# A two-layer kernel whose engine orders are written out as a table of streams, with new planned durations

## Chip, core and metric

The kernel runs on one core of one Trainium2 chip. The metric is device time in microseconds (us), as the median of several executions. TensorE is called PE, VectorE DVE, ScalarE ACT, GpSimd POOL and SyncE SP, as in the profile.

## What is computed

Input is x of shape (4, 1024, 128), that is 4096 tokens of 128 numbers, and the weights of two layers. Each layer normalises x once and adds an attention part and a feed-forward part of the same normalised tensor to x:

```python
xn = layernorm(x)
x = x + rwkv6_attention(xn) + moe_ffn_0(xn)      # first layer
xn = layernorm(x)
x = x + causal_attention(xn) + looped_moe(xn)    # second layer
```

- The recurrent attention (4 heads, key width 64, value width 128) mixes each token with the one before it through five small products, and then runs the recurrence `S = exp(w_t) * S + k_t v_t`.
- `moe_ffn_0` cuts every token into 8 pieces of 16, takes the best 2 of 16 experts for each and applies gelu between two products.
- The causal attention has 16 heads of width 8 with one shared key and value head, over 1024 tokens in each of 4 batches.
- `looped_moe` is run twice: rms-norm, a router, the best 2 of 8 experts (128 to 256 to 128, silu gate), and a sum.

## The kernel before

Everything stays in fp32 or in exact splits into bf16 parts. The work of each layer is written as many **streams**: Python generators, one for each part of the work on each engine. Every generator yields, ahead of each step, the planned start of that step, and `merge` (L63) takes the generators of one engine and always advances the one whose next planned start is smallest. So the planned starts set the order of the instructions on PE, ACT, DVE, POOL and SP. Between the two layers all five queues meet (`k.meet`).

**Where the planned starts come from.** `first_layer` (L2178) and `second_layer` (L2416) describe every step to a `Plan` (L2068): the engine, the stream, a key, a wished time, a duration (`takes`), the steps that it needs, and which PSUM banks it fills or frees. `Plan.run` (L2089) then plays the plan through: again and again it picks the engine that can start soonest and, on it, among the heads of the streams that can start within a small slack, the one with the smallest wish. The result gives the starts (`FIRST` and `AT` in the code) and the bank of every use (`plan.place`).

- The first layer works in four turns of 1024 tokens (`plan_mixtures`, `plan_levels`, `plan_carry`, `plan_gated`), 0 to about 548 us of the trace. Beside them run 256 gelu tiles: PE forms each with two products (L482), ACT applies gelu (L528), PE reduces (L494), DVE weighs (L543), POOL adds (L582).
- In each turn a recurrence of levels runs between PE and DVE. DVE scales (L1121, L1126), PE fills the banks of a level (a small product at L650 and then L737, L764 or L779), and DVE places the result (L1064).
- The mixtures of a turn: PE L673, DVE `rw_mix` L1008, POOL `rw_mix` L1158, then the products L685, L691, L707, L720. POOL also clears `rw_full` once (L1164, step `zero`).
- The second layer holds attention and experts side by side. Attention has a pass for the maxima (PE L2718 and L2736, DVE L2764 or L2761) and one for the sums (PE L2863 and L2840, ACT exp L2887, PE L2826). Experts: PE L3109, L3125, L3141, L3157, ACT L3186, L3198, L3208, DVE L3218, L3232.
- The experts' results go to memory, POOL gathers them (L3049), and DVE adds them to `zt` (L3244, L3249).
- At the start of the second layer DVE turns constants into bf16 (L1821, step `cast`), and `ap_value` (L1980) takes a product from the banks.
- PE works in several tile shapes (128x128, 128x32, 64x128, 32x128 and so on). The plan charges 0.1 us for each change of shape (`TILE_SWITCH`) and 1.3 us for each change of ACT's function table.

## Time and profile before

| | us |
|---|---|
| median of 3 executions | 1351.98 |
| lowest and highest | 1349.23 and 1352.38 |
| profiled execution, first to last instruction (span) | 1317.6 |
| PE busy | 1206.5 (92% of the span) |
| DVE busy | 1050.7 (80%) |
| ACT busy | 891.2 (68%) |
| POOL busy | 482.3 (37%) |

The profile gives the span of its execution; what lies around the span isn't in it, and the median of the three executions is 34.4 us above it. Busy time counts the instructions of an engine; the releaser of a wait is the instruction that ended it. The granted clock is the share of full speed that PE was given.

### The profile page before, as it was taken

The numbers are of one execution on the slowest core, as the hardware profiler recorded it, in microseconds if no ns is written. First come the engines' busy times: TensorE is split into PE (matmuls) and PEld (weight loads), VectorE is DVE, ScalarE is ACT, GpSimd is POOL, SyncE is SP. The second block draws the span as 40 slices with busy tenths as digits, with TensorE's granted clock in tenths as the row PEclk, the third lists the DMA queues.
The fourth block names the chain that finished last, engine by engine and source line by source line (L and its number), as shares of the span: only waits on it lengthen the run. The fifth ranks groups of instructions, "written<-read, shape, count | busy, mean of one in ns | idle before, by whom it ended". The sixth has DMA issues, their size and how long they took to land. (4 is left out here: it accounts for less than half of the span.)

```text
span 1317.6 us, 28397 instructions
## 1 busy us (share of the span) xinstructions
PE 1206.5 (92%) x11172; PEld 593.3 (45%) x11172; DVE 1050.7 (80%) x1954; ACT 891.2 (68%) x1246; POOL 482.3 (37%) x446
## 2 busy tenths in 40 slices
PE   6888998899988989798899999999899999999988
PEld 3333332333433323365555555555456544555434
DVE  4589789869898779769977799778787798787863
ACT  3668997898877888643266676666666666666666
POOL 3542554345514872320155511555025550000170
PEclk8889998999999999989999999999999999999999
DMA  6333322233332343248364544556335453233020
GB/s 224 116 117 125 106 94 101 92 109 101 100 103 94 111 132 106 93 118 233 106 183 136 174 122 117 151 139 157 87 101 160 133 142 89 72 82 105 19 64 28
DMA packets 129876, 152.88 MB, mean 116 GB/s; under 512 B 16048, under 2 KB 90800, under 8 KB 129616
## 3 DMA queue, kind: packets, MB, share of 16 engines
q1 hardware_dynamic: 111104, 127.50, 32.9%
q0 software_dynamic: 8192, 16.79, 4.3%
q10 hardware_dynamic: 10448, 6.77, 1.7%
q8 instruction: 89, 1.46, 0.5%
q14 instruction: 43, 0.35, 0.1%
HBM read 109.20 MB, written 41.81 MB: 115 GB/s over the span
## 5 line engine op out<-in xcount | busy, mean ns | idle before, releaser
L2887 ACT ACTIVATE ax_prob<-second_pair 128x1024 f32<-128x1024 f32 (+1 forms) x320 | 292.9, 939 | 146.4 <-PE second_pair L2840 94.4
L528 ACT ACTIVATE m_act_h<-first_pair,const 128x1024 f32<-128x1024 f32 x256 | 270.1, 1114 | 57.7 <-PE first_pair L482 44.1
L2764 DVE TENSOR_REDUCE am_top<-second_pair 128x2 f32<-128x1024 f32 (+1 forms) x192 | 222.9, 1175 | 38.6 <-PE second_pair L2718 25.5
L3019 POOL DMA_INDIRECT slot_tokens<-xn,mr_slots x128 | 124.0, 969 | 273.7 <-PE second_bank L1877 86.2
L3049 POOL DMA_INDIRECT m_back<-slot_results,mr_slots x128 | 122.2, 955 | 243.2 <-PE second_pair L2718 167.7
L482 PE MATMUL first_pair<-m_terms,w1s 96*128 96x512 bf16 x512 | 145.9, 391 | 19.6 <-ACT m_act_h L528 19.4
L2826 PE MATMUL ax_sums<-ax_prob,al_vs 128*32 128x512 f32 (+3 forms) x1536 | 161.2, 500 | 1.8 <-ACT ax_prob L2887 1.6
L494 PE MATMUL first_pair<-m_act_h,const 128*32 128x512 f32 x1024 | 130.4, 610 | 7.0 <-DVE m_prod L543 4.9
L582 POOL TENSOR_TENSOR m_both<-m_prod,m_both 128x512 f32<-128x512 f32 x64 | 86.7, 1371 | 123.8 <-DVE m_both L543 123.8
L2863 PE MATMUL second_pair<-al_qs,al_ks 51*128 51x512 bf16 (+3 forms) x768 | 115.9, 329 | 12.8 <-DVE am_top L2764 4.3
L2718 PE MATMUL second_pair<-al_ks,al_qs 48*128 48x512 bf16 (+3 forms) x768 | 116.2, 327 | 7.6 <-DVE am_top L2764 3.7
L482 PEld LDWEIGHTS first_pair<-m_terms,w1s 96*128 96x128 bf16 x512 | 38.4, 99 | 136.7 <-ACT m_act_h L528 75.3
L2863 PEld LDWEIGHTS second_pair<-al_qs,al_ks 51*128 51x128 bf16 x768 | 32.9, 93 | 103.8 <-issue 48.0
L2764 DVE TENSOR_REDUCE am_later<-second_pair 128x2 f32<-128x768 f32 (+1 forms) x64 | 68.6, 1085 | 6.4 <-PE second_pair L2736 6.1
L3141 PE MATMUL second_pair<-m_tok,m_wt 128*128 128x256 f32 (+1 forms) x244 | 66.8, 361 | 2.1 <-DVE m_act L3218 1.0
L2718 PEld LDWEIGHTS second_pair<-al_ks,al_qs 48*128 48x128 bf16 x768 | 33.5, 93 | 62.4 <-issue 30.9
L494 PEld LDWEIGHTS first_pair<-m_act_h,const 128*32 128x32 f32 x1024 | 25.9, 110 | 77.4 <-issue 46.3
L3157 PE MATMUL second_bank<-m_wt,m_hid 128*128 128x128 f32 x364 | 60.0, 295 | 0.8 <-DVE m_hid L3232 0.7
L3125 PE MATMUL second_bank<-m_tok,m_wt 128*128 128x256 f32 (+1 forms) x216 | 58.2, 364 | 2.2 <-DMA m_wt<-in_experts 1.6
L1158 POOL TENSOR_TENSOR rw_mix<-rw_mix,xn 128x512 f32<-128x512 f32 x40 | 48.5, 1235 | 23.5 <-DVE rw_mix L1008 23.4
L543 DVE SCALAR_TENSOR_TENSOR m_both<-first_pair,const,m_share 128x512 f32<-128x512 f32 x64 | 46.6, 741 | 11.8 <-PE first_pair L494 10.9
L543 DVE SCALAR_TENSOR_TENSOR m_prod<-first_pair,const,m_share 128x512 f32<-128x512 f32 x64 | 46.8, 740 | 10.5 <-issue 7.8
(396 smaller groups left out, 2515.1 us busy)
## 6 DMA issues: line engine op xcount, KB each, us to landing
m_wt<-in_experts SPq DMA_DIRECT2D x96, 384.0 KB
m_share<-shares SPq DMA_DIRECT2D x128, 256.0 KB
m_rows<-slot_tokens SPq DMA_DIRECT2D x60, 128.0 KB
slot_results<-m_y SPq DMA_DIRECT2D x60, 128.0 KB
stack<-mp_part SPq DMA_DIRECT2D x48, 128.0 KB
m_terms<-stack SPq DMA_DIRECT2D x64, 96.0 KB, 3.7
qstack<-ap_qpart SPq DMA_DIRECT2D x48, 128.0 KB
al_qs<-qstack SPq DMA_DIRECT2D x32, 192.0 KB, 3.9
```

What stands on the lines that cost most here:

```text
L482: p = E.matmul(banks.bank("up", n, ep)[:, j, :], self.w1s[:, (4 * half + ep) * P:(4 * half + ep + 1) * P], self.terms[:, q % slots, :], st ...
L494: p = E.matmul(banks.bank("down", n, j)[32 * ep:32 * ep + 32, :], self.w("w2", 32 * (4 * half + ep), 32 * (4 * half + ep) + 32), self.act_ ...
L528: A.activation(self.act_h[:, slot, :, :], banks.bank("up", n, ep)[:, :, :], ACT.Gelu, bias=self.w("b1", 4 * half + ep, 4 * half + ep + 1)) ...
L543: V.scalar_tensor_tensor(self.product(pair, half, j)[:, :], banks.bank("down", n, j), self.w("b2", half, half + 1), self.share[:, q % slot ...
L582: G.tensor_tensor(both[:, :], self.prod[j][:, :], both[:, :], ALU.add).then_inc(self.folded, 1)
L2718: p = E.matmul(banks.bank("max", i, m)[:, x, first:first + n], *self.keys_queries(i, blk, a, x, seg, n), start=a == pairs[0], stop=True, s ...
L2764: V.tensor_reduce(into[:, 2 * a:2 * a + 2, at], tile[:, :, 0:n], AX, ALU.max, negate=True).then_inc(*banks.empties("max", i, m))
L2826: p = E.matmul(self.sums[VW * h:VW * h + VW, off:TILE], self.loads.vs[:, b % 2, blk, :], self.prob[:, g % 3, h, off:TILE], start=blk == 0, ...
L2863: p = E.matmul(tile[:, x, first:first + n], self.loads.ks[rows, b % 2, blk * CH:(blk + 1) * CH], self.loads.qs[rows, i % Q_SLOTS, a, th * ...
L2887: A.activation(dst, src, ACT.Exp, scale=SCALE).then_inc(*banks.empties("sum", i, u))
L3019: G.indirect_dma_start(self.tokens[g], bass.IndirectOffsetOnAxis(ap=self.route.slots[g][second][:, i:i + 1], axis=0), self.entry.zn(GC * g ...
L3049: G.indirect_dma_start(self.back[q % 2][:, n, m, :], None, self.results[ph], bass.IndirectOffsetOnAxis(ap=self.route.slots[g][n][:, c * NC ...
```

## The change

The plan's steps, streams and needs stay, and every instruction stays. What changes:

1. `Plan.run` takes an `orders` table: for each engine a string in which each letter names the stream that takes the next step on that engine (a for the first stream declared, b for the second, and so on). Wishes, slack and patience no longer choose. `FIRST_ORDERS` spells out the first layer and `SECOND_ORDERS` the second.
2. Some 30 planned durations are set to other values, and two planned needs are added (the first load of the attention waits for `zero`, the products for the maxima for `cast`). They no longer choose the order; they move the planned starts along it, and through these the choice of PSUM banks.

```diff
+ENGINES = ["PE", "ACT", "DVE", "POOL", "SP"]
+NAMES = "abcdefghijklmnopqrstuvwxyzABCDEFGHIJKLMNOPQRSTUVWXYZ"
...
-    def run(self):
-
+    def run(self, orders=None):
+
+        spelled = collections.defaultdict(list)
+        for engine, stream in self.streams:
+            spelled[engine].append((engine, stream))
+        turns = {engine: [spelled[engine][NAMES.index(name)] for name in order] for engine, order in (orders or {}).items()}
+        taken = collections.Counter()
...
             for (engine, stream), n in heads.items():
+                if orders and turns[engine][taken[engine]] != (engine, stream):
+                    continue
...
-            engine = min(best, key=lambda e: min(best[e])[0])
+            engine = min(sorted(best, key=ENGINES.index), key=lambda e: min(best[e])[-1] if orders else min(best[e])[0])
+            taken[engine] += 1
...
+FIRST_ORDERS = {
+    "PE":
+        "affaffghgahhigcccigccbajcccgccddkccddccjddcjcjccddcckcackcdccdecbcacddcckcdccddcckcacddcckckdeccddclcecclkccddcckclddllcfmmcbfaccffccddgccec"
...
-    return p.run(), p
+    return p.run(FIRST_ORDERS), p
...
-            pe("levels", ("lev", it, h), at, 1.7 if h < 32 else 1.0, ready, ("zero",), *(ago("outs", 1) if h == 32 else []), lag=0.3, fills=1, uses=[("lev", it, h, s) for s in range(2)])
+            pe("levels", ("lev", it, h), at, 0.87 if h < 32 else 1.0, ready, ("zero",), *(ago("outs", 1) if h == 32 else []), lag=0.3, fills=1, uses=[("lev", it, h, s) for s in range(2)])
...
-        dve("low", ("mixed", it, s), at, 1.24, ("delta", it, s), *([("low", it, 0, 1)] if s else ago("state", NC)), port=True)
+        dve("low", ("mixed", it, s), at, 0.68, ("delta", it, s), *([("low", it, 0, 1)] if s else ago("state", NC)), port=True)
...
-        dve("turn", ("parts", i), end, 1.6, ("rows", i), *([("sent", i - 2)] if i > 1 else []))
+        dve("turn", ("parts", i), end, 1.05, ("rows", i), *([("sent", i - 2)] if i > 1 else []))
...
-            act("exp", ("exp", i, u), wish, {384: 0.75, 128: 0.52}.get(n, 0.95), ("sum", i, u),
+            act("exp", ("exp", i, u), wish, {384: 0.7, 128: 0.49}.get(n, 0.91), ("sum", i, u),
...
-    return p.run(), p
+    return p.run(SECOND_ORDERS), p
```

The order moves on every engine. Three places follow. The lines of the changed kernel stand one higher up to L2060 of the old one, and 75 higher behind the tables.

**POOL, mixtures of the first turn** (`rw_mix` is the mixture, `rw_full` the buffer that is cleared, `mp_` the router of the feed-forward part). Before:

```order
L291 TENSOR_TENSOR mp_h<-mp_h,mp_part 128x512
L294 TENSOR_TENSOR mp_part<-mp_h,mp_part 128x512
L1163 MEMSET rw_carry 128x128
L1164 MEMSET rw_full 128x4096
L1158 TENSOR_TENSOR rw_mix<-rw_mix,xn 128x512 x2
L357 TENSOR_TENSOR mp_logits<-mp_logits,mp_peak 128x512
L1158 TENSOR_TENSOR rw_mix<-rw_mix,xn 128x512 x2
```

After the change:

```order
L1159 TENSOR_TENSOR rw_mix<-rw_mix,xn 128x512 x4
L358 TENSOR_TENSOR mp_logits<-mp_logits,mp_peak 128x512
L361 TENSOR_TENSOR mp_one<-mp_one,mp_eq 128x512
L1159 TENSOR_TENSOR rw_mix<-rw_mix,xn 128x512 x2
L365 TENSOR_TENSOR mp_one<-mp_one,mp_logits 128x512
L369 TENSOR_TENSOR mp_one<-mp_one,mp_sum 128x512
L1159 TENSOR_TENSOR rw_mix<-rw_mix,xn 128x512
L292 TENSOR_TENSOR mp_h<-mp_h,mp_part 128x512
L295 TENSOR_TENSOR mp_part<-mp_h,mp_part 128x512
L1164 MEMSET rw_carry 128x128
L1165 MEMSET rw_full 128x4096
```

Clearing `rw_carry` and `rw_full` stood ahead of the first mixtures, and now stands behind the mixtures of the first turn but three.

**PE, second turn, from the fill of one level to the fill of the next** (`rw_selves` with `rw_key` or `rw_low` are fills; `m_terms` and `m_act_h` belong to the gelu tiles). Before:

```order
L650 MATMUL first_pair<-bf_ident 32x1
L737 MATMUL first_pair<-rw_selves,rw_key 32x64 x32
L482 MATMUL first_pair<-m_terms,w1s 128x512 x4
L494 MATMUL first_pair<-m_act_h,const 32x512 x4
L650 MATMUL first_pair<-bf_ident 32x1
L737 MATMUL first_pair<-rw_selves,rw_low 32x64 x32
```

After the change:

```order
L651 MATMUL first_pair<-bf_ident 32x1
L738 MATMUL first_pair<-rw_selves,rw_key 32x64 x32
L483 MATMUL first_pair<-m_terms,w1s 128x512 x2
L238 MATMUL first_pair<-xn,const 128x512
L483 MATMUL first_pair<-m_terms,w1s 128x512 x4
L495 MATMUL first_pair<-m_act_h,const 32x512 x4
L483 MATMUL first_pair<-m_terms,w1s 128x512 x2
L495 MATMUL first_pair<-m_act_h,const 32x512 x4
L483 MATMUL first_pair<-m_terms,w1s 128x512 x4
L651 MATMUL first_pair<-bf_ident 32x1
L738 MATMUL first_pair<-rw_selves,rw_low 32x64 x32
```

Between the two fills there were 8 products, and there are now 21.

**DVE, near the end of the second layer** (`am_top` and `am_later` reduce scores from PSUM, `m_back` are gathered results, `ao_` belongs to the output projection). Before:

```order
L3259 TENSOR_TENSOR zt<-zt,x 128x512
L2764 TENSOR_REDUCE am_top<-second_pair 128x2
L2764 TENSOR_REDUCE am_later<-second_pair 128x2
L3244 SCALAR_TENSOR_TENSOR zt<-m_back,mr_share,zt 128x128 x4
L3249 SCALAR_TENSOR_TENSOR zt<-m_back,mr_share,zt 128x128 x4
L2764 TENSOR_REDUCE am_later<-second_pair 128x2
L2954 RECIPROCAL ao_inverse<-second_bank 128x16
L2956 TENSOR_TENSOR ao_scaled<-second_bank,ao_inverse 128x128
L2768 TENSOR_TENSOR am_top<-am_top,am_later 128x4x4
L2787 CAST am_part<-am_rows 32x128
L2789 TENSOR_TENSOR am_restm<-am_rows,am_part 32x128
```

After the change:

```order
L2843 TENSOR_TENSOR am_top<-am_top,am_later 128x4x4
L3029 RECIPROCAL ao_inverse<-second_pair 128x16
L3031 TENSOR_TENSOR ao_scaled<-second_pair,ao_inverse 128x128
L2862 CAST am_part<-am_rows 32x128
L2864 TENSOR_TENSOR am_restm<-am_rows,am_part 32x128
L2866 CAST am_part<-am_restm 32x128
L2868 TENSOR_TENSOR am_part<-am_restm,am_part 32x128
L3029 RECIPROCAL ao_inverse<-second_bank 128x16
L3031 TENSOR_TENSOR ao_scaled<-second_bank,ao_inverse 128x128
L3319 SCALAR_TENSOR_TENSOR zt<-m_back,mr_share,zt 128x128 x4
L3324 SCALAR_TENSOR_TENSOR zt<-m_back,mr_share,zt 128x128 x4
L3319 SCALAR_TENSOR_TENSOR zt<-m_back,mr_share,zt 128x128 x4
```

Before, the additions of gathered results (L3244, L3249) stood ahead of a score reduction (L2764) and of the step that ends the maxima (L2768 to L2793). Now the last score reductions stand ahead of the first row shown (L2843 is the old L2768), and the additions (L3319, L3324) behind all of them.

## Rows read from the trace of the kernel before

**Rows 1.** The page's head: busy time, share of the span, instructions.
```profile
PE 1206.5 (92%) x11172; PEld 593.3 (45%) x11172; DVE 1050.7 (80%) x1954; ACT 891.2 (68%) x1246; POOL 482.3 (37%) x446
```

**Rows 2.** Five stretches: length, busy of each engine, granted clock, DMA share, GB/s.
```profile
0.00:66.00 66.00, 48.45 (x261) 22.48 (x269) 34.54 (x64) 31.80 (x44) 29.81 (x26) 0.87 0.54 170
66.00:528.00 462.00, 418.62 (x4144) 157.95 (x4142) 394.37 (x759) 380.24 (x431) 218.58 (x181) 0.98 0.32 106
528.00:660.00 132.00, 112.13 (x731) 71.11 (x730) 108.48 (x227) 55.65 (x110) 23.55 (x21) 0.96 0.48 138
660.00:1254.00 594.00, 574.85 (x5491) 318.76 (x5489) 484.62 (x832) 380.25 (x608) 186.66 (x196) 1.00 0.44 120
1254.00:1317.60 63.60, 52.44 (x565) 23.01 (x557) 28.70 (x76) 43.24 (x54) 23.74 (x25) 0.95 0.17 45
```

**Rows 3.** PE's waits from 66 to 528 us: total, times, longest.
```profile
PE first_pair L482 <- ACT m_act_h L528: 17.3, 40, 1.6
PE first_pair L650 <- DVE rw_low L1126: 7.0, 4, 3.1
PE first_pair L494 <- DVE m_prod L543: 4.9, 3, 2.7
```

**Rows 4.** PE in order of time: start, us, instruction, [idle before <-releaser].
```profile
58.37 0.60 PE L482 MATMUL first_pair<-m_terms,w1s 96*128 96x512 bf16 x2 [0.40 <-ACT m_act_h L528]
```

**Rows 5.** PE between two level fills, second turn.
```profile
218.87 1.06 PE L494 MATMUL first_pair<-m_act_h,const 128*32 128x512 f32 x8
223.00 0.18 PE L650 MATMUL first_pair<-bf_ident 64*32 64x1 bf16 x1 [3.06 <-DVE rw_low L1126]
```

**Rows 6.** DVE in the same stretch.
```profile
219.21 2.55 DVE L1121 SCALAR_TENSOR_TENSOR rw_selves<-rw_pre,const,rw_rec 128x256 f32<-128x256 f32 x2
221.69 1.25 DVE L1126 TENSOR_TENSOR rw_low<-rw_suf,rw_key 128x256 f32<-128x256 f32 x1
...
225.48 1.66 DVE L1121 SCALAR_TENSOR_TENSOR rw_selves<-rw_pre,const,rw_rec 128x256 f32<-128x256 f32 x4
```

**Rows 7.** POOL in the same stretch.
```profile
217.79 2.51 POOL L582 TENSOR_TENSOR m_both<-m_prod,m_both 128x512 f32<-128x512 f32 x2
```

**Rows 8.** DVE groups by line: busy, mean ns of one, idle before.
```profile
L1121 DVE SCALAR_TENSOR_TENSOR rw_selves<-rw_pre,const,rw_rec 128x256 f32<-128x256 f32 x96 | 51.6, 585 | 0.0
```

**Rows 9.** PE in the second layer, score products and an expert's product.
```profile
1100.01 0.38 PE L2718 MATMUL second_pair<-al_ks,al_qs 48*128 48x512 bf16 x2
1100.23 0.38 PE L2863 MATMUL second_pair<-al_qs,al_ks 51*128 51x512 bf16 x2
1100.54 1.16 PE L3157 MATMUL second_bank<-m_wt,m_hid 128*128 128x128 f32 x8
```

**Rows 10.** ACT's table loads at the gelu.
```profile
L528 ACT ACT_TABLE_LOAD x16 | 20.5, 1283 | 0.3
```

**Rows 11.** POOL in the first turn's mixtures.
```profile
41.66 3.50 POOL L1164 MEMSET rw_full<- 128x4096 f32 x1
45.13 2.35 POOL L1158 TENSOR_TENSOR rw_mix<-rw_mix,xn 128x512 f32<-128x512 f32 x2
```

**Rows 12.** PE, the product that waits for them.
```profile
46.49 1.12 PE L685 MATMUL first_pair<-rw_mix,const 128*128 128x512 f32 x2 [2.09 <-POOL rw_mix L1158]
```

**Rows 13.** DVE behind the start of the second layer.
```profile
559.09 0.23 DVE L1821 CAST bf_earlier_t<-const 128x128 bf16<-128x128 f32 x1 [0.89 <-DMA const<-in_const]
```

**Rows 14.** PE in the same stretch.
```profile
561.86 1.92 PE L1885 MATMUL second_pair<-ax_y,const 128*32 128x512 f32 x2 [3.68 <-DVE ap_value L1980]
```

**Rows 15.** DVE near the end.
```profile
1267.54 1.14 DVE L3244 SCALAR_TENSOR_TENSOR zt<-m_back,mr_share,zt 128x128 f32<-128x128 f32 x4 [2.66 <-DMA m_back<-slot_results,mr_slots]
...
1269.64 1.22 DVE L2764 TENSOR_REDUCE am_later<-second_pair 128x2 f32<-128x1024 f32 x1
```

**Rows 16.** PE near the end.
```profile
1270.92 0.39 PE L2863 MATMUL second_pair<-al_qs,al_ks 51*128 51x512 bf16 x2 [2.25 <-DVE am_later L2764]
...
1274.04 1.93 PE L2826 MATMUL ax_sums<-ax_prob,al_vs 128*32 128x512 f32 x8 [0.61 <-ACT ax_prob L2887]
```

More of the change, by code:

```diff
@@ L2256, in plan_units @@
             if half:
-                pool("pair", ("pair", pair, j), at + DOWN_AFTER, 1.3, ("product", n, j))
+                pool("pair", ("pair", pair, j), at + DOWN_AFTER, 1.26, ("product", n, j))
         if n % 4 == 3:
@@ L2320, in plan_levels @@
         dve("scales", ("self", it, h), at, 0.4, ("bonus", it), *ago("lev64", 1), lag=0.15, port=True)
-    pe("levels", ("lev", it, 0), at, 2.2, ("self", it, NH - 1), *ago("fill_a"), lag=0.3, fills=1, uses=[("lev", it, 0, s) for s in range(2)])
+    pe("levels", ("lev", it, 0), at, 1.12, ("self", it, NH - 1), *ago("fill_a"), lag=0.3, fills=1, uses=[("lev", it, 0, s) for s in range(2)])
     for s in range(2):
@@ L2342, in plan_levels @@
     for half in range(2):
-        pe("levels", ("lev64", it, half), at, 1.25, ("scale", it, 64, 2), lag=0.3, fills=1, uses=[("lev64", it, half, s) for s in range(2)])
+        pe("levels", ("lev64", it, half), at, 0.97, ("scale", it, 64, 2), lag=0.3, fills=1, uses=[("lev64", it, half, s) for s in range(2)])
         for s in range(2):
@@ L2379, in plan_gated @@
     for s in range(2):
[L2380 to L2381 removed]
+        dve("gn", ("gngate", it, s), at, 0.67, ("affine", it, s), lag=0.2, port=True)
+        pe("gn", ("go", it, s), at, 0.88, ("gngate", it, s), lag=0.3, fills=1)
     for s in range(2):
@@ L2522, in plan_route @@
             dve("route", ("zn", ph, c), at, 1.1, ("invert", ph))
-        pe("route", ("turned", ph, c), at, 0.75, ("zn", ph, c) if loop else ("scale", GC * g + c), *before, lag=0.25, fills=1)
+        pe("route", ("turned", ph, c), at, 0.5, ("zn", ph, c) if loop else ("scale", GC * g + c), *before, lag=0.25, fills=1)
         act("route", ("turnedc", ph, c), at, 0.48, ("turned", ph, c), *before, frees=("turned", ph, c))
```

102 lines of the change are left out of this document (79 added, 23 removed).

## The prediction

> **What bounds the kernel now.** I read the head of the page first. PE is busy for 1206.5 us of a span of 1317.6 us, DVE for 1050.7 and ACT for 891.2 [rows 1]. No instruction goes away with this change, so it can win PE's idle time, which is 111.1 us, and the time lost to a lower clock, and little else. The table of stretches says where these lie [rows 2]. Each figure is length less PE's busy time:
>
> - 0 to 66 us (normalisation, first mixtures): 17.5 us idle.
> - 66 to 528 us (first layer): 43.4 us idle, granted clock 0.98.
> - 528 to 660 us (the layers meet, the second starts): 19.9 us idle, clock 0.96.
> - 660 to 1254 us (second layer): 19.2 us idle in 594, clock 1.00.
> - 1254 us to the end: 11.2 us idle, clock 0.95.
>
> So the second layer's long middle is bound by PE, and better order has little to find there. In the first layer no engine is full: PE 418.6, DVE 394.4 and ACT 380.2 of 462 us. There the order itself is the limit.
>
> PE's list of waits for the first layer shows two kinds [rows 3]. The first is the gelu: 17.3 us in 40 waits. The order of time shows one. Two products take 0.60 us, one gelu more than that, so a tile formed directly behind others waits 0.40 us for its bank [rows 4]. The second kind is the chain of levels: 7.0 us in only 4 waits in front of L650. The longest shows the mechanism. PE has 8 products between two fills and is done at 219.93, then idles 3.06 us [rows 5]. DVE meanwhile needs 2.55 us for two L1121 and 1.25 us for one L1126, while four L1121 take 1.66 us a little later [rows 6]. POOL works without a break in the slow stretch [rows 7]. So a DVE step between SBUF operands can take some three times its time beside POOL (1.28 us each against 0.42). Over all 96 the mean is 585 ns [rows 8], 170 ns above the 415 of the undisturbed ones, 16 us in total.
>
> **The change, part by part.** The letters spell the same steps, and on every engine the count of instructions of each operation is the same; only ACT's table loads differ. Costs and gains are counted against the profiled execution (span 1317.6). The median of the runs is 34.4 us above that span, and I carry this over unchanged.
>
> *Changes of tile shape.* Counting over the whole order of PE, from shape to shape, the first layer goes from 298 to 338 changes, the second from 735 to 686. A price is in the trace: products with 64 rows start 0.22 us apart, and the last of them before a 128x128 product 0.31 us apart, so 0.09 us for a change [rows 9]. That makes +3.6 and -4.4 us. The Trainium skill (TensorEngine Tiling (Array Packing), Key Properties) says that changing the tiling mode drains the engine; it gives no price, and by that rule alone the first layer would pay for each of its 40 new changes and the time there would rise by those 3.6 us.
>
> *Table loads.* ACT has 42 before and 37 now, all five in the first layer, at 1.28 us each [rows 10]: 6.4 us less on ACT. ACT has 82 us idle there, so I cost it at nothing beside the next term. If gelu were the bound it would be worth the 6.4.
>
> *Start.* POOL clears `rw_full` for 3.50 us and only then makes the first mixtures [rows 11]. PE waits 2.09 us for these [rows 12]. The new order has the mixtures first. I take -2 us, between 0 (the next wait takes its place) and -4. What is late next is `rw_full`, which the steps that place the levels need, later in the turn.
>
> *Gelu waits.* I count the tiles whose two products stand directly behind another tile's: 106 of 256 before, 82 now, 23% fewer. 23% of 17.3 us is 4 us. Bounds 0 and -9 (half).
>
> *Level chain.* Between the fills of the levels of one turn PE now has 757 products instead of 590, over the four turns. At the place that waited 3.06 us it has 21 instead of 8. These waits should nearly go: -6 us of 7.0. Bounds +4 (one gap now holds 2 products, one 5, and each can wait what the longest waits now) and -7.
>
> *The other waits of the first layer.* 43.4 less 17.3 and 7.0 leaves 19.1 us in small waits for DVE, POOL and ACT. I see no single place there, and take a third, -6. Bounds 0 and -12.
>
> *Clock.* A share of 0.02 of 462 us is 9.2 us lost, 0.04 of 132 us is 5.3, and 0.05 of 63.6 is 3.2 [rows 2]. The drops follow stalls, so fewer stalls give back some: -3 in the first layer; those behind it are in the next terms.
>
> *Meeting of the layers.* DVE takes its bf16 constants when their load lands, at 559.09 us, and L1980 stands behind them [rows 13]. PE waits 3.68 us for L1980, with two L1885 in a row, and then takes 1.92 us for one of them, in a stretch of lower clock [rows 14]. In the new order PE has eleven products of the experts and the router between `ap_value`'s product and L1885. -5 us, bounds 0 and -8.
>
> *Middle of the second layer.* 19.2 us of idle time in 594: -3, bounds +6 and -8.
>
> *End.* DVE stands at the addition of gathered results for 2.66 us, with a score reduction behind it [rows 15]. PE waits 2.25 us for that reduction and then takes 1.93 us for eight L2826, twice the time of full clock [rows 16]. The new order has these reductions and the end of the maxima ahead of the additions: -4 us, bounds 0 and -7.
>
> The sum is -2 + 3.6 - 4.4 - 4 - 6 - 6 - 3 - 5 - 3 - 4 = -33.8 us. A removed wait can return at the next place: PE that comes earlier meets the next late producer, here DVE, busy for 85% of the first layer. Of the 30 us of idle time that I take out I give a third back, +10; the third is my choice, between none and all. That leaves -24: a span near 1294 and a median of **1328 us**.
>
> **Rivals.**
>
> *Nearly all of it returns.* The waits move from the old places to new ones, and only the changes of shape remain (-0.8 us): 1351 us. For it: ACT and DVE are over 80% busy in the first layer. Against it: the two structural stalls, DVE behind a gather and POOL behind a memset, have nothing to take their place.
>
> *More is found.* A search over orders for all engines together could halve the idle time behind 66 us, 93.7 us, and with it half of the 17.7 us of clock: -47 -9 + 10 = -46, or 1306 us. Against it: the middle of the second layer has hardly any.
>
> *Slower: DVE beside POOL.* The new plan takes lower times for DVE steps that share with POOL (0.68 for 1.24, 0.67 for 0.9). If PE's order is now cut to DVE steps at full speed, each stretched step is waited for. Of the chains of levels the whole stretch of 16 us (L1121 alone) would show on PE, where 7.0 of waits show now: +9. With the changes of shape in the first layer (+3.6), and two stalls as long as today's longest at the gaps of 2 and 5 products (+6), it comes to +19 with no gain elsewhere: 1371 us. It decides if PE's idle time in the first layer rises above 43.4 us by more than what start, meeting and end give (11). Against it: the gaps grew where the chain waited. The Trainium skill (SBUF — State Buffer, section "SBUF: two separate sides") calls the port pair that DVE and GpSimd share an exclusive lock for a whole instruction. By that rule a DVE step waits out a POOL step; the trace agrees, with 1.28 us against 0.42 beside POOL steps of 1.26.
>
> That the change does nothing is excluded: nearly every row of every engine's order moves.
>
> **How the numbers follow.** A difference below 0.3% (4 us) can't be told from none here. Forecast, 1310 to 1347: 0.65. More is found: 0.15. Nearly all returns: 0.09. Slower: 0.11. The likeliest gives 1328. The range must leave out no more than 2 in 10: from 1304, which takes in most of the larger gain, to 1352, which takes in the case of no change and leaves out the slower one. Faster 0.80, same 0.09, slower 0.11.
>
> **What would show it.** In the profile of the changed kernel: PE's idle time in the first layer near 30 us; waits of L651 under 3 us in total; no wait of PE for POOL's mixtures; no DVE wait for a gather with a score reduction behind it; granted clock 0.99 or more there; PE's busy time within some 10 us of 1206. If PE's idle time is as before, with new waits for DVE at L651 or for gelu at L483, the forecast is wrong and the second or the last rival holds.

## The result, and the profile after

| | before | changed |
|---|---|---|
| median, us | 1352.18 (4 executions, 1349.23 to 1360.16) | 1303.38 (4 executions, 1300.2 to 1305.22) |
| ratio | | 0.9641 [0.9605, 0.9677] |
| profiled execution, its own time | not recorded | 1300.2 |
| its span | 1317.6 | 1298.7 |

The kernel became 48.8 us faster, twice the 24 us of the forecast, and 0.6 us below the range. The direction was right, and the size nearest to the rival "more is found" (1306).

The table holds a trap. The changed kernel's time is its span plus 1.5 us. For the kernel before I had taken 34.4 us as lying around the span. No execution with both numbers shows such a gap: two later ones of the kernel before, on two chips, have spans of 1323.8 and 1322.3 and times of 1325.56 and 1324.12 us, so 1.8 us lie there. The span of 1317.6 belongs to a quicker execution than the three that were timed. One and the same program (before) had a median of 1320.48, 1322.71 and 1354.95 us on three chips, and the lowest of its 15 times on the slowest of these was 1345.63; so the first profile of before most likely comes from a quicker chip than its timed executions. So the two first profiles can't be subtracted (that gives 19 us, the timed runs give 49), and what follows compares traces of one chip.

The head of the changed kernel's page, against [rows 1]:

```profile
span 1298.7 us, 28395 instructions
PE 1200.2 (92%) x11172; PEld 596.1 (46%) x11172; DVE 1065.6 (82%) x1954; ACT 878.3 (68%) x1241; POOL 489.1 (38%) x446
```

Its first four stretches, against [rows 2] (columns as there):

```profile
0.00:66.00 66.00, 52.38 (x282) 24.30 (x282) 42.32 (x70) 33.30 (x47) 29.73 (x27) 0.90 0.58 179
66.00:528.00 462.00, 424.75 (x4194) 158.74 (x4194) 398.39 (x754) 379.75 (x430) 218.14 (x176) 0.97 0.32 105
528.00:660.00 132.00, 114.21 (x713) 72.97 (x713) 122.27 (x245) 55.17 (x119) 37.88 (x35) 0.97 0.54 155
660.00:1254.00 594.00, 574.54 (x5643) 323.74 (x5645) 488.07 (x842) 383.48 (x616) 187.05 (x194) 1.00 0.41 118
```

PE's idle time in the first layer is 37.3 us, 43.4 before. In 660 to 1254 us it is the same 19.5 us, but 5643 products fit where 5491 did. PE's waits of the first layer, against [rows 3]:

```profile
PE first_pair L495 <- DVE rw_diag L1065: 5.9, 5, 3.1
PE first_pair L651 <- DVE rw_mix L1009: 4.7, 1, 4.7
PE first_pair L794 <- DVE m_prod L544: 2.7, 1, 2.7
PE first_pair L651 <- DVE rw_diag L1065: 2.6, 2, 1.6
```

No gelu stands among the first: of the 17.3 us in front of L482, 0.7 are left. DVE steps took the head of the list, one of 4.7 us at the level chain among them.

### The profile page after: what moved, and what is told of

The parts are those of the page before. It is cut to its first block, busy times and chain, and to the rows that moved or that the text cites. A ratio compares the mean times of both kernels' runs of the same rounds, so it can differ in the third digit from the quotient of the medians.

```text
span 1298.7 us, 28395 instructions
## 1 busy us (share of the span) xinstructions
PE 1200.2 (92%) x11172; PEld 596.1 (46%) x11172; DVE 1065.6 (82%) x1954; ACT 878.3 (68%) x1241; POOL 489.1 (38%) x446
## 4 chain that ended last, share of the span: by engine, by line
PE 53%; DVE 13%; ACT 3%; issue 3%; POOL 1%; DMA 0%; DVEq 0%; SPq 0%; ACTq 0%
PE ax_sums L2901 10%; PE second_pair L2938 6%; PE second_pair L2793 5%; PE first_pair L495 3%; PE second_pair L3216 3%; PE second_bank L3232 3%; DVE am_top L2839 3%; PE second_bank L3200 2%; PE first_pair L483 2%; PE second_pair L3200 2%; PE second_pair L3232 2%; PE second_bank L3216 2%; PE second_pair L2915 2%; ACT ax_prob L2962 1%; PE second_pair L2811 1%
## 5 line engine op out<-in xcount | busy, mean ns | idle before, releaser
L529 ACT ACTIVATE m_act_h<-first_pair,const 128x1024 f32<-128x1024 f32 x256 | 273.9, 1117 | 60.9 <-PE first_pair L483 49.0
L2901 PE MATMUL ax_sums<-ax_prob,al_vs 128*32 128x512 f32 (+3 forms) x1536 | 156.8, 501 | 0.4 <-ACT ax_y L2977 0.3
L483 PE MATMUL first_pair<-m_terms,w1s 96*128 96x512 bf16 x512 | 147.1, 392 | 4.1 <-ACT m_act_h L529 2.8
L495 PE MATMUL first_pair<-m_act_h,const 128*32 128x512 f32 x1024 | 135.7, 618 | 10.6 <-DVE rw_diag L1065 5.9
L2938 PE MATMUL second_pair<-al_qs,al_ks 51*128 51x512 bf16 (+3 forms) x768 | 112.9, 331 | 11.4 <-ACT ax_prob L2962 7.1
L2793 PE MATMUL second_pair<-al_ks,al_qs 48*128 48x512 bf16 (+3 forms) x768 | 112.7, 330 | 11.3 <-DVE am_top L2839 2.6
L483 PEld LDWEIGHTS first_pair<-m_terms,w1s 96*128 96x128 bf16 x512 | 37.9, 99 | 130.0 <-ACT m_act_h L529 60.0
L2938 PEld LDWEIGHTS second_pair<-al_qs,al_ks 51*128 51x128 bf16 x768 | 32.4, 94 | 81.7 <-issue 32.8
L2793 PEld LDWEIGHTS second_pair<-al_ks,al_qs 48*128 48x128 bf16 x768 | 33.1, 93 | 79.2 <-issue 31.5
L3216 PE MATMUL second_pair<-m_tok,m_wt 128*128 128x256 f32 (+1 forms) x244 | 64.1, 354 | 0.6 <-ACT ao_turned L3049 0.4
L495 PEld LDWEIGHTS first_pair<-m_act_h,const 128*32 128x32 f32 x1024 | 24.7, 110 | 75.6 <-issue 45.5
L3200 PE MATMUL second_pair<-m_tok,m_wt 128*128 128x256 f32 (+1 forms) x208 | 54.0, 350 | 2.3 <-ACT ax_y L1905 1.4
L2901 PEld LDWEIGHTS ax_sums<-ax_prob,al_vs 128*32 128x32 f32 x1536 | 35.2, 109 | 44.0 <-issue 29.5
L2915 PE MATMUL second_pair<-bf_earlier_t,bf_ident 64*128 64x128 bf16 (+2 forms) x384 | 53.7, 218 | 0.4 <-issue 0.4
```

What stands on the lines that cost most here:

```text
L483: p = E.matmul(banks.bank("up", n, ep)[:, j, :], self.w1s[:, (4 * half + ep) * P:(4 * half + ep + 1) * P], self.terms[:, q % slots, :], st ...
L495: p = E.matmul(banks.bank("down", n, j)[32 * ep:32 * ep + 32, :], self.w("w2", 32 * (4 * half + ep), 32 * (4 * half + ep) + 32), self.act_ ...
L529: A.activation(self.act_h[:, slot, :, :], banks.bank("up", n, ep)[:, :, :], ACT.Gelu, bias=self.w("b1", 4 * half + ep, 4 * half + ep + 1)) ...
L2793: p = E.matmul(banks.bank("max", i, m)[:, x, first:first + n], *self.keys_queries(i, blk, a, x, seg, n), start=a == pairs[0], stop=True, s ...
L2901: p = E.matmul(self.sums[VW * h:VW * h + VW, off:TILE], self.loads.vs[:, b % 2, blk, :], self.prob[:, g % 3, h, off:TILE], start=blk == 0, ...
L2938: p = E.matmul(tile[:, x, first:first + n], self.loads.ks[rows, b % 2, blk * CH:(blk + 1) * CH], self.loads.qs[rows, i % Q_SLOTS, a, th * ...
```

## The experiments

Twelve kernels in three groups, each group on one chip with the kernel before beside it. A ratio is the median over that of the kernel before on the same chip, with its 95% interval. Line numbers of changed kernels are 1 higher in the first layer's code and 75 higher in the second's (L482 is L483, L2863 is L2938).

**Undoing the change by parts.** On the first chip the kernel before took 1320.48 us (13 executions).

`c1_before`: no edit, a control.

> The kernel before, unchanged, as a control. Its first profile had a span of 1317.6 us, 34.4 below the median of its runs, where the changed kernel's time is only 1.5 us above its span. Theory A: the first profile caught an untypically short execution, and a new one has a span within 3 us of the median, near 1350, with 25 us or more of extra idle time on PE. Rival B: time outside the span; then the new span is again near 1318 and the time near 1352.

Measured: 1322.5 us, ratio 1.0004 [0.9977, 1.0032], span 1323.8. Rival B fell: 1.8 us lie around the span. Of theory A the span near the median held, the level of 1350 did not.

`c2_first_only`: the first layer's table and durations, the second layer as before.

```diff
@@ first_layer
-    return p.run(), p
+    return p.run(FIRST_ORDERS), p
@@ second_layer
     return p.run(), p
```

> The new order and durations in the first layer only; the second layer is ordered as before. The first layer ended at 547.6 us in the old profile and at 541.9 in the new one, the rest gained 13 us. Theory A (the gain lies in both layers as the profiles show, and the old execution's extra 30 us lies in one of them): if in the first layer, this is 1352 - 36 = 1316 us; if in the second, 1346 us. Rival: the layers depend on each other and this is slower than 1352.

Measured: 1306.02 us, 0.9880 [0.9816, 0.9944]. The second layer's first product starts at 532.25 us, at 551.58 in the control: 19.3 us, all of it in the first layer (spans 1304.2 and 1323.8). By the medians the kernel gained 14.5 us; the control's profiled execution was its longest.

`c3_second_only`: the other half.

```diff
@@ first_layer
     return p.run(), p
@@ second_layer
-    return p.run(), p
+    return p.run(SECOND_ORDERS), p
```

> The new order and durations in the second layer only. If the extra 30 us of the old kernel lies in the second layer: 1352 - 43 = 1309 us; if in the first: 1352 - 13 = 1339 us.

Measured: 1280.58 us, 0.9712 [0.9649, 0.9775], span 1275.8. That is 2.9%, nearly two and a half times the first layer's 1.2%. The expected times of both halves rested on the level of 1352 and can't be held against these. The product of the two ratios is 0.9596, and the whole change gives 0.9606 to 0.9641: the halves add up.

`c4_durations_only`: all new durations and needs, no table; each engine chooses by wishes and starts as before. The diff is against the changed kernel.

```diff
@@ first_layer
-    return p.run(FIRST_ORDERS), p
+    return p.run(), p
@@ second_layer
-    return p.run(SECOND_ORDERS), p
+    return p.run(), p
```

> The new durations and needs, without the tables: wishes choose the order, as before. Theory: the wishes were fitted to the old durations, so the order found is no better: 1352 us within 1% either way. Rival: the gain comes from true durations, and this kernel has half of it or more, 1328 us or less.

Measured: 1340.49 us, 1.0151 [1.0089, 1.0213]. The new durations alone cost 20 us, somewhat more than the 1% that I allowed, and the rival is out. That the wishes had been tuned with the old durations would explain it; no run tests this.

**Order, banks, and single places.** On the second chip the kernel before took 1354.95 us (15 executions).

`d1_after`: the changed kernel, a control.

> The changed kernel again, as a control, on a chip beside the kernel before, so that the two traces can be laid side by side. Theory 'the first profile of before came from a quicker chip than its runs, and nothing lies outside the span': both kernels' times are their spans plus 1.5 to 2 us here, and the ratio is 0.964 again (0.958 to 0.970); with the kernel before near 1320 us this one takes 1268 to 1279. Rival 'some 34 us lie outside the span of the kernel before': its time exceeds its span by 30 us or more and this one's does not.

Measured: 1304.89 us, 0.9606 [0.9573, 0.9638]; profiled execution 1312.16 us, span 1310.8. The ratio stands, the gap around the span is 1.4 us. The kernel before stood at 1355 us here and not near 1320, so the level that I had expected for the changed one doesn't apply.

`d2_orders_only`: the tables with the old durations and without the two new needs; one of the lines, against the changed kernel:

```diff
-        pe("h", ("h", i), at, 0.88, *ago("lo"), lag=0.25, fills=1)
+        pe("h", ("h", i), at, 0.96, *ago("lo"), lag=0.25, fills=1)
...
```

> The two tables, with the old durations in the plan and without the two new needs (the memset before the first load, the cast before the maxima). With the order written out, durations decide only which PSUM bank a step gets. Theory 'the order is the whole gain': the time stays within 0.5% of the changed kernel's on the same chip. Rival 'the banks matter, since a step waits for the one that had its bank': 1% to 2.5% slower than the changed kernel, and more waits of PE for the reader of a bank (the gelu's in the first layer, the exponentials' in the second).

Measured: 1314.33 us, 0.9688 [0.9656, 0.9719], 0.7% above the changed kernel. That lies between the two theories. The order is four fifths of the gain (41 of 50 us). The rest comes with the durations and needs, which under a table leave the order as it is and move the choice of banks. The rival's sign is there too: PE's idle time in front of the gelu's product L483 is 14.4 us, 5.4 in `d1_after` and 22.8 in `d4_start_end`, which has the old order on PE; in front of the two score products (L2938 and L2793) it is 27.7 us against 24.4. So about half of what went at the gelu went with the orders, and half with the banks.

`d3_first_205us`: the second layer's table for its first 205 us alone.

```diff
-                if orders and turns[engine][taken[engine]] != (engine, stream):
+                if orders and (upto is None or taken[engine] < upto[engine]) and turns[engine][taken[engine]] != (engine, stream):
...
+    return p.run(SECOND_ORDERS, {'PE': 419, 'ACT': 194, 'DVE': 232, 'SP': 119, 'POOL': 69}), p
```

> In the second layer the table holds for the first 205 us alone (419 of PE's steps, 194 of ACT's, 232 of DVE's, 119 of SP's, 69 of POOL's); behind them each engine chooses by the old rules and durations. First layer as before. In the run with the second layer's table alone this stretch, from the layer's first product to the first group's last gathered addition, took 206 us against 223 before on the same chip. Theory 'the gain of the second layer sits at its start and its end, about 17 us each': 12 to 20 us less than before, ratio 0.985 to 0.991, all of it in that stretch. Rival 'what is won at the start is given back as soon as the order is free again': within 4 us of before.

Measured: 1351.01 us, 0.9951 [0.9916, 0.9986], 3.9 us under the kernel before. My theory fell and the rival held. The stretch did shorten, to 209.7 us from the layer's first product to the group's last gathered addition, against 228.8 in the next kernel, which has the old order there. PE had done the same work by then, 1515 and 1514 products (the row ends at the milestone), of the experts and of the attention alike:

```profile
557.11:766.80 209.69, 194.72 (x1515) 123.67 (x1516) 189.18 (x353) 110.74 (x212) 79.91 (x78) 0.98 0.59 167
562.66:791.50 228.84, 207.70 (x1514) 124.85 (x1516) 185.99 (x357) 112.08 (x210) 79.12 (x78) 0.94 0.55 155
```

So the lead of 19 us was real. But the rest of the layer took 582.7 us here and 567.4 there: 15 of the 19 us were given back where the old rules choose the order. With the whole table the rest gains as well: between `c1_before` and `c3_second_only` the stretch shortened by some 17 us and what lies behind it by 28.

`d4_start_end`: the order of before written out step for step, with two places moved, the two single stalls that the forecast had named.

```diff
-        "bbaeeceecceecbeebeedcdcccddbb
+        "bbeeceecceeacbeebeedcdcccddbb
...
-        "ggjkgjgkggggjggkgggghgjmgkmmggggmgggngggglggmgogglgmghlmmlnommmmmnmmmono",
+        "ggjkgjgkggggjggkgggghgjmgkmmggggmgggnggggggmggggmglhlmmonlommlmmmnmmmono",
```

> The order of before written out as a table, step for step, with two moves alone: in the first layer POOL clears rw_full behind the first six mixtures instead of ahead of them, and at the end of the second DVE adds the gathered results behind the last score reduction, not between. Nothing else moves on any engine. By the forecast's terms these are worth 2 us and 4 us: ratio 0.994 to 0.997, no wait of PE for the first mixtures, none for the reduction near the end. Rival 'a wait taken out returns at the next late producer': within 2 us of before, with a new wait of nearly the same length behind each. Rival 'local order at these two places is worth more, since the whole end shortened by 17 us in the run of the second layer alone': 10 us or more.

Measured: 1358.29 us, 1.0023 [0.9991, 1.0056]. Nothing was won. PE in this kernel, in order of time, at the first mixtures and behind them:

```profile
45.36 1.56 PE L56 MATMUL first_pair<-shared 128*128 128x384 f32 x4 [1.13 <-DVE rw_mix L1009]
...
63.90 1.09 PE L253 MATMUL first_pair<-shared,mp_one 128*128 128x128 f32 x4 [3.76 <-POOL mp_one L369]
```

And POOL beside it:

```profile
56.84 2.14 POOL L1159 TENSOR_TENSOR rw_mix<-rw_mix,xn 128x512 f32<-128x512 f32 x2 [1.23 <-DVE rw_mix L1009]
58.92 0.20 POOL L1164 MEMSET rw_carry<- 128x128 f32 x1
59.06 3.51 POOL L1165 MEMSET rw_full<- 128x4096 f32 x1
62.53 1.23 POOL L369 TENSOR_TENSOR mp_one<-mp_one,mp_sum 128x512 f32<-128x512 f32 x1
```

The 2.09 us in front of the mixtures' product [rows 12] are gone; the 3.5 us of memset now stand ahead of the router's last step (L369), and PE waits 3.76 us for that. On a POOL that has work queued a moved step doesn't vanish. At the end DVE's additions stand behind the reductions as meant, but pauses that no step explains (last section) fall into that stretch of this trace, so the end alone isn't settled. Both together pay nothing: "nearly all of it returns" holds at the first place and for the two together, though not for the table.

**Whose order?** On the third chip the kernel before took 1322.71 us (19 executions).

`e1_before`: no edit, so that there is a trace of this chip.

> The kernel before, profiled beside the others of this call, so that a chip's own share can be told from the change's. On one chip its runs had a median of 1320 us, on another 1355, with one and the same program. Theory 'chips differ, the changes of the order keep their ratio': 0.997 to 1.003 against itself, span 1.5 to 2 us under its time, and whatever the level here the ratio of the kernel with the swap is 0.955 to 0.968. Rival 'the first profile's gap of 34 us lies around the span': time less span of 30 us or more.

Measured: 1323.4 us, 1.0017 [0.9990, 1.0043], span 1322.3, which is 1.8 us under the time of that execution. The theory held.

`e2_after_swap`: the changed kernel with the first three transposes of the second layer in another order on PE, and ACT's first two steps.

```diff
-        "babkalkcllm
+        "aabbklkcllm
...
-        "cakkjcjd
+        "ackkjcjd
```

> The changed kernel with one wait taken out: PE begins the second layer with the two transposes of x, whose input is there, and the transpose of zt comes third instead of first (ACT's first two steps change places with it). In the changed kernel PE stands 2.2 us at that first transpose of zt. Theory 'PE bounds here': that wait falls under 1 us and the rest of the layer starts 1 us earlier, which the runs can't tell from the changed kernel's 0.9606 to 0.9641. Rival 'it returns at the next producer', as the 2.1 us at the first mixtures came back as 3.8 us at POOL's next step: new waits of 2 us or more within 10 us behind it.

Measured: 1265.16 us, 0.9575 [0.9548, 0.9602]. PE at the start of the second layer:

```profile
536.48 0.66 PE L1792 MATMUL second_bank<-shared,x 128*128 128x128 f32 x4 [0.84 <-DVEq L60]
...
541.41 0.70 PE L3200 MATMUL second_pair<-m_tok,m_wt 128*128 128x256 f32 x2 [1.75 <-DMA m_wt<-in_experts]
```

The first product waited 2.20 us in the changed kernel (`d1_after`) and waits 0.84 now. But the two transposes of `zt` that follow wait 0.19 and 0.37 us, and the product behind them waits 1.75 us for the expert's weights, 1.00 in the control. 1.4 us were taken out and 1.3 came back within 5 us, which is the rival, with smaller waits than it named. The interval overlaps the control's on the second chip, so the lower ratio isn't shown to be the swap's.

`e3_first_pe_only`: in the first layer PE alone follows its table.

```diff
-                if orders and turns[engine][taken[engine]] != (engine, stream):
+                if engine in turns and turns[engine][taken[engine]] != (engine, stream):
...
-    return p.run(), p
+    return p.run({e: FIRST_ORDERS[e] for e in ['PE']}), p
```

> First layer: PE alone follows its new table; ACT, DVE, POOL and SP choose by the old rules with the old durations. Second layer as before. Theory 'the gain comes from the streams of all engines fitted to each other': no gain here, PE waits for ACT and DVE steps that come in an order made for the old PE: ratio 1.00 to 1.03, with the waits at the gelu (21 us of idle time at the first products before, 5 us with the whole table) back above 12 us. Rival 'PE's order carries the gain, the others follow by themselves': 0.985 to 0.992, as with the whole table of the first layer (0.988).

Measured: 1342.62 us, 1.0152 [1.0113, 1.0190]. The gelu's waits are back, and new ones for DVE beside them:

```profile
L483 PE MATMUL first_pair<-m_terms,w1s 96*128 96x512 bf16 x512 | 152.6, 400 | 23.9 <-ACT m_act_h L529 18.1 <-DVE rw_diag L1054 2.4 <-DVE m_prod L544 1.6
L495 PE MATMUL first_pair<-m_act_h,const 128*32 128x512 f32 x1024 | 136.2, 620 | 11.6 <-DVE rw_diag L1065 5.9 <-DVE m_prod L544 4.1 <-DVE rw_gate L1020 0.7
```

PE's order is here that of the changed kernel, but for 8 of 4528 products that have changed places with a neighbour. So it isn't PE's spacing of the tiles alone that removes the wait for the gelu; the other engines' orders have to match. This kernel has the old durations too, as has `d2_orders_only`, where all engines follow the table and the gelu's product has 14.4 us: the step from 23.9 to 14.4 is the orders' (on two chips), the one from there to some 5 the durations'.

`e4_second_pe_only`: the same in the second layer (with one need more, for the constants' load).

```diff
-    return p.run(), p
+    return p.run({e: SECOND_ORDERS[e] for e in ['PE']}), p
```

> Second layer: PE alone follows its new table, the others choose by the old rules and durations (DVE's values wait for the constants' cast, so that the load is there). First layer as before. Theory 'PE is busy for 97% of this layer's middle, so its own order decides': 0.971 to 0.980, near the 0.971 of the whole table of the second layer. Rival 'the streams must fit on ACT and DVE too': 0.99 to 1.01, with waits of PE at the score products (13.7 us before, 1.9 us with the whole table) of 10 us or more.

Measured: 1316.86 us, 0.9950 [0.9920, 0.9980]. PE's order alone brings a sixth of the second layer's 0.029. The second layer of this kernel, cut at its first product:

```profile
553.30:1320.00 766.70, 712.16 (x6644) 412.59 (x6644) 607.85 (x1113) 465.35 (x756) 233.36 (x238) 0.98 0.44 120
```

PE is busy 12.1 us less than in `e1_before` (724.25) and idle 8.5 us more (54.5 for 46.1). So PE's own order does make its work shorter, and nearly all of that goes into new waits while ACT and DVE keep their old orders. The old durations are in this kernel as well; `d2_orders_only` prices these at 0.7% for both layers, so most of the difference to 0.971 is the other engines' orders.

## Where the time went

The third chip has both sides: the control (span 1322.3) and the changed kernel with the swap (1263.7), 58.6 us apart. Each was cut at the second layer's first product, so that both rows of a layer hold the same 4528 and 6644 products. First the kernel before:

```profile
0.00:552.00 552.00, 487.36 (x4528) 187.32 (x4528) 442.05 (x837) 423.78 (x488) 250.16 (x208) 0.96 0.34 110
552.00:1322.30 770.30, 724.25 (x6644) 406.26 (x6644) 609.20 (x1118) 466.87 (x758) 231.99 (x238) 0.99 0.43 120
```

Then the changed one with the swap:

```profile
0.00:536.40 536.40, 489.61 (x4528) 188.74 (x4528) 449.40 (x837) 418.96 (x482) 254.13 (x208) 0.95 0.35 113
536.40:1263.70 727.30, 701.80 (x6644) 408.60 (x6644) 612.38 (x1117) 459.82 (x759) 235.21 (x238) 0.99 0.45 127
```

| us | idle time of PE | busy time of PE | sum |
|---|---|---|---|
| first layer | 64.6 to 46.8, -17.8 | 487.4 to 489.6, +2.3 | -15.6 |
| second layer | 46.1 to 25.5, -20.6 | 724.3 to 701.8, -22.5 | -43.0 |

In the first layer the shape of the sum was right. In the second, PE's idle time is nearly halved, and its busy time falls by as much again, for the same products. The swap has no part in this: the first chip's pair, with the table in the second layer alone, splits the same way (46.0 to 23.1 us idle, 726.2 to 703.9 busy):

```profile
551.58:1323.80 772.22, 726.22 (x6644) 408.02 (x6644) 610.60 (x1117) 467.26 (x758) 231.60 (x238) 0.98 0.43 119
548.88:1275.80 726.92, 703.85 (x6644) 410.18 (x6644) 611.23 (x1113) 459.62 (x759) 234.01 (x238) 0.99 0.45 127
```

PE's largest groups, before:

```profile
L482 PE MATMUL first_pair<-m_terms,w1s 96*128 96x512 bf16 x512 | 145.4, 391 | 21.5 <-ACT m_act_h L528 21.2
L494 PE MATMUL first_pair<-m_act_h,const 128*32 128x512 f32 x1024 | 134.0, 626 | 6.4 <-DVE m_prod L543 3.8 <-DVE rw_diag L1064 1.4 <-ACT m_act_h L528 0.9
L2863 PE MATMUL second_pair<-al_qs,al_ks 51*128 51x512 bf16 (+3 forms) x768 | 116.3, 330 | 13.5 <-DVE am_top L2764 4.7 <-DVE am_later L2764 4.4 <-ACT ax_prob L2887 2.6
```

and with the tables (and the swap):

```profile
L483 PE MATMUL first_pair<-m_terms,w1s 96*128 96x512 bf16 x512 | 147.3, 392 | 5.1 <-ACT m_act_h L529 3.7 <-DVE m_prod L544 0.6 <-issue 0.2
L495 PE MATMUL first_pair<-m_act_h,const 128*32 128x512 f32 x1024 | 134.6, 616 | 9.9 <-DVE rw_diag L1065 6.6 <-DVE rw_gate L1020 1.7 <-DVE m_prod L544 1.0
L2938 PE MATMUL second_pair<-al_qs,al_ks 51*128 51x512 bf16 (+3 forms) x768 | 111.2, 328 | 1.6 <-ACT ax_prob L2962 0.7 <-DVE am_top L2839 0.6
```

The idle time behind the last bar is the reading: the gelu's product from 21.5 to 5.1 us, the score product L2863 from 13.5 to 1.6. These two groups are 28.3 of the 38.4 us of idle time. The second of them depends on the chip: in both traces of the changed kernel where engines stand still for no reason in the program (last section) L2938 keeps 11.4 and 11.8 us.

The 22.5 us of busy time in the second layer have three sources that the traces price. The prices are estimates from the durations in the traces; no run changes one of the three alone:

- *Drains in front of waits.* A wait costs more than the idle time listed for it. Groups of products with an idle gap behind them take 0.14 us longer to their end than groups of the same form without one (68 such groups before, 33 after, over all forms): 9.6 us and 4.4, so -5.2. The gaps themselves went from 76 to 38.
- *Changes of tile shape.* Counted in the traces from group to group they go from 735 to 686, as counted in the order. In the trace of `c1_before` an expert's two products of 128x256 (L3141) take 0.60 us behind most other products of full shape and 0.70 behind a product of another shape, a score product for one, so 0.1 for a change: -4.9.
- *Clock.* The stretch to 660 us has 0.95 in 108 us before and 0.97 in 123.6 us after, the last 68 us 0.95 and 0.99: 5.4 + 3.4 against 3.7 + 0.7, so -4.4. This one isn't shown to be the change's: the kernel before in `c1_before` has 0.91 up to 660 us, so two executions of one kernel differ by as much. The rows of these stretches, first of before:

```profile
552.00:660.00 108.00, 92.15 (x567) 61.48 (x568) 92.69 (x206) 41.88 (x91) 18.65 (x17) 0.95 0.57 159
660.00:1254.00 594.00, 574.65 (x5481) 320.30 (x5479) 484.54 (x835) 378.79 (x610) 186.61 (x195) 1.00 0.44 121
1254.00:1322.30 68.30, 57.44 (x601) 24.48 (x599) 31.97 (x79) 46.20 (x57) 26.73 (x28) 0.95 0.17 45
```

and of the changed kernel with the swap:

```profile
536.40:660.00 123.60, 109.05 (x737) 74.69 (x738) 116.18 (x238) 54.39 (x120) 35.89 (x32) 0.97 0.61 175
660.00:1195.30 535.30, 529.67 (x5194) 303.87 (x5193) 455.91 (x792) 352.66 (x573) 167.74 (x174) 1.00 0.44 125
1195.30:1263.70 68.40, 63.07 (x719) 30.03 (x715) 40.28 (x89) 52.77 (x67) 31.58 (x32) 0.99 0.19 51
```

That is 14.5 us. For most of the other 8 `e4_second_pe_only` gives the place: PE's order alone took out 12.1 us of busy time, with 68 gaps where there were 76, so the new sequence of products on PE is worth more than the 4.9 counted as changes of shape. An estimate agrees: taking for each pair of neighbouring products the mean distance of their starts over five traces of the first and third chip, the old order adds up to 705.6 us and the new one to 693.9. With these 11.7 in place of the 4.9 the three sources make 21.3 of the 22.5.

## Why the prediction was right and wrong, step by step

The step that failed is in the first paragraph of the prediction and in the term for the second layer that follows from it: the change "can win PE's idle time ... and little else", and in the second layer's middle "better order has little to find". The terms behind the first layer (-4.4, -5, -3, -4) come to 16.4 us, and the second layer gained 43.0 on the third chip: 20.6 of idle and 22.5 of busy time. The term +10, a third given back, made it worse. Part by part:

- **"The median of the runs is 34.4 us above that span, and I carry this over unchanged."** Failed: 1.8 us lie there. It cost the forecast little, since the timed executions of before and after stood on one level, on which every term is 2 to 3% larger.
- **First layer** (-2 start, +3.6 shapes, -4 gelu, -6 chain, -6 other waits, -3 clock: -17.4). Measured -19.3 on the first chip, -15.6 on the third, but from other parts. PE's waits for ACT from 66 to 528 us, on the third chip, went from 20.7 to 2.7 us, and those for DVE rose from 20.9 to 26.0.
  - *Gelu -4*: 21.5 to 5.1, -16.4; four times as much, beyond my bound of -9. The count of tiles directly behind others, down by 23%, was no measure of the wait: `e3_first_pe_only` has the new PE order and 23.9 us, and about half of the fall came with the banks (`d2_orders_only`), for which the prediction had no term.
  - *Table loads 0*: five fewer in all, as read, but six fewer in the first layer and one more in the second; `d2_orders_only` has the 37 loads too and 14.4 us at the gelu, so what they are worth by themselves stays open.
  - *Level chain -6*: L650 had 10.0 us of idle time on the third chip and L651 has 7.5, so -2.5; four waits for L1126 (6.8 us) went, others for `rw_diag` and `rw_add` came (and one of 4.7 us for `rw_mix` in the first profile). More products between two fills did end the longest waits for L1126; what took their place are steps of other chains.
  - *Other waits -6*: all told PE's idle time from 66 to 528 us fell from 43.6 to 30.9 us, 12.7, less than the gelu's part alone, so the others rose, L495 by 3.5 and L794 by 2.4.
  - *Start -2*: right, L685 waited 2.1 us and L686 waits 0.
  - *Shapes +3.6*: not shown; busy time went up by 2.3 us on the third chip and down by 1.6 on the first. The Trainium skill (TensorEngine Tiling (Array Packing), Key Properties) says that a change of tiling mode drains the engine, and by that rule alone each of the 40 new changes is paid; the traces agree as far as a product behind one of another shape takes some 0.1 us longer.
  - *Clock -3*: not found, the granted clock from 66 to 528 us is 0.97 on the third chip before and after, and 0.96 to 0.98 in all traces of either kernel.
- **Meeting of the layers -5.** L1885's wait of 2.7 us is gone, but new ones for the expert's weights and `ax_y` came; PE's idle time of 528 to 660 us goes from 19.9 to 16.8: -3.
- **"Middle of the second layer ... -3"**, since "better order has little to find there". This is the step that failed most. Idle time in 660 to 1254 us was 19.4 of 594; with the tables it is 5.6 of 535 (660 to 1195 us). I read a PE at 97% as bound and took its busy time as fixed. The waits were short but many, 14 us of them could go, and the busy time held drains and costly changes from one product to the next: PE's order alone took 12.1 us out of it. On the second chip, where engines stand still for other reasons, less idle time went: against `d4_start_end`, which has the old order but for two places, the second layer of `d1_after` has 45.2 us for 59.7, and 712.6 us of busy time for 736.6.
- **End -4.** From 10.9 to 5.3 us of idle time in the last 68, -5.5, and the clock from 0.95 to 0.99, -2.7. The term held both, so it is -8.2, beyond the bound of -7; the idle time alone is near the forecast.
- **"Of the 30 us of idle time that I take out I give a third back, +10."** Failed for the table: PE's idle time fell by 38 us in all. It is true for single moves, where more than a third came back (`d4_start_end`: everything). That a table for all engines at once has these second waits already in its account is my reading; no run shows it. Without this term the sum was -33.8; what is missing to the -58.6 of the third chip is the second layer, in idle and in busy time.
- **The tests.** PE's idle time in the first layer near 30 us: 37.3 in the first profile, 30.9 on the third chip. L651 under 3 us: failed, 7.5. No wait for POOL's mixtures: right. No DVE wait for a gather with a score reduction behind it: right, DVE's waits for gathers (six, 15.4 us) are gone in the first profile. Clock 0.99: failed. Busy time within 10 us of 1206: right in the first profile (1200.2), and an accident; on one chip it fell by 20 (1211.6 to 1191.4).
- **The rivals.** "More is found" took half of the 93.7 us of idle time as won; 38.4 were on the third chip, in all. It was the nearest, and partly by luck: its idle time came out smaller, its other source, the clock, gave at most 4.4, and the busy time, which it didn't count, gave 22.5. "Slower, DVE beside POOL": waits for `rw_diag`, a DVE step, did grow (6.6 us at L495, 1.4 before), but DVE's L1121 kept its 590 ns (595 now) and the price stayed small. The Trainium skill (SBUF — State Buffer, "SBUF: two separate sides") says that whichever of DVE and GpSimd has their shared ports keeps them for its whole instruction; the mean of L1121 shows that the change neither added to such waits nor took from them, and no run tests more. The lower durations that the plan gives such steps set no order once a table does: DVE's order is the same in `d1_after` and `d2_orders_only`.

## What to carry to other kernels

Put the time of a profiled execution beside its span before anything is built on the difference, and compare traces of one chip only. An engine that is 97% busy isn't at its limit: short waits lengthen the work in front of them, and which products are neighbours changes the busy time itself, so count the waits as well as their length. A stall with work queued on every side can't be priced alone: here two moved steps, PE's order alone and the table for a quarter of a layer brought between -0.5% and +1.5%, and the same steps ordered on all engines together -4%. And an order that is ahead after one stretch has won nothing until what follows it fits too: 15 of 19 us went back in `d3_first_205us`.

## What the runs showed of the hardware

One program differs by 2.6% between chips (1320 and 1355 us), and the difference isn't spread over the run. In the changed kernel's trace of the second chip PE has done 3586 products at 450 us, with the swap on the third chip 3604. In the next 50 us it does 500 here (second chip):

```profile
450.00:500.00 50.00, 45.97 (x500) 14.34 (x498) 38.93 (x88) 39.27 (x40) 22.43 (x21) 0.97 0.40 129
```

and 662 there (third chip):

```profile
450.00:500.00 50.00, 49.05 (x662) 14.83 (x664) 42.78 (x92) 44.47 (x46) 23.40 (x21) 1.00 0.43 139
```

Inside that stretch 64 products of one line, which start without a gap elsewhere, come in pieces on the second chip:

```profile
477.39 0.71 PE L738 MATMUL first_pair<-rw_selves,rw_low 64*32 64x64 f32 x43
478.55 0.32 PE L738 MATMUL first_pair<-rw_selves,rw_low 64*32 64x64 f32 x4 [0.46 <-issue]
479.31 0.34 PE L738 MATMUL first_pair<-rw_selves,rw_low 64*32 64x64 f32 x5 [0.44 <-issue]
```

Near the end, in the trace of `d4_start_end`, PE, DVE and ACT stand still together for 3 to 4 us, with nothing in the program that ends it:

```profile
1287.56 1.23 DVE L2839 TENSOR_REDUCE am_top<-second_pair 128x2 f32<-128x1024 f32 x1 [3.11 <-remote]
1287.51 1.73 ACT L2962 ACTIVATE ax_prob<-second_pair 128x1024 f32<-128x1024 f32 x2 [3.94 <-remote]
1288.59 0.50 PE L2793 MATMUL second_pair<-al_ks,al_qs 48*128 48x384 bf16 x2 [3.36 <-ACT ax_prob L2962]
```

The traces of the second chip and the changed kernel's first have such waits that end by nothing in the program; those of the first and third chip and the first of before have none. The ratio depends on it little, if at all: 0.9606 on the slow chip, 0.9575 with the swap on the third, and 0.9596 as the product of the two halves on the first; the changed kernel without the swap was never run on a quick chip. What stops the engines stays open; no run was aimed at it.
